# Fused attention and sparse FFN layer: another order of the first pair's row maxima, and feature products on another engine

## The chip, the cores and the metric

The kernel runs on one core of one Trainium2 chip. The metric is the device time of one execution, in microseconds; the median of three runs of the kernel before is 409.96 us (409.67 to 410.95). The engines of a core run their own instruction streams and meet at semaphores: TensorE (PE), VectorE (DVE), ScalarE (ACT), GpSimd (POOL) and SyncE (SP, here only DMA issue).

## The reference

The layer has 1024 tokens of width 256, 16 heads of 16 dimensions, and 8 "splats" per head. Attention is computed twice, with plain scores and with guided scores (plain plus a term from splat features), and the two outputs are blended. A feed-forward layer with 2:4 sparsity follows.

```python
q, k, v = heads(x @ Wq.T), heads(x @ Wk.T), heads(x @ Wv.T)
scores = einsum('bhid,bhjd->bhij', q, k) / sqrt(hd)
std_out = out_proj(softmax(where(mask, scores, neg)))
diff  = x[:, :, :, None, :] - splat_positions                # of q and of k
gauss = exp(-0.5 * sum(diff * diff, -1) / scales ** 2)
dirp  = tanh(einsum('bhsnd,hnd->bhsn', diff, dirn))
splat_attn = einsum('bhin,bhjn->bhij', amp * qg, kg) + strength * einsum(..., amp * qg * qd, kg * kd)
gsa_out = out_proj(softmax(where(mask, scores + sensitivity * splat_attn, neg)))
x = layernorm(x + (1 - blend) * std_out + blend * gsa_out)
h = silu(x @ w_gate) * (x @ w_up);  x = layernorm(x + keep_2_of_4(h) @ w_down)
```

## The kernel before

Matrix products use float32r parts: a value is split into a high part and a low part, and three products (lines 743 to 745) make one. The 16 heads are worked on in 8 pairs. A matrix of 128 rows holds 8 heads, so the first four pairs come from "chunk" 0 and the last four from chunk 1. For each chunk c, for q and k (w = 0, 1) and for both halves of the tokens (hf = 0, 1) there are a projection ("proj"), a Gaussian part ("gauss") and a directional part ("dirp"). A feature is made in five steps. PE makes gauss and dirp, ACT takes exp and tanh of them (L654, L662), DVE multiplies them (L1088 for q, with a factor, and L1091 for k), ACT rounds the product to its high part (L618) and DVE subtracts that to have the low part (L1099). Features 0 to 3 are those of chunk 0, and 4 to 7 those of chunk 1. DMAs (`stack`, L378) then put base parts and features of one head into rows of `q_st` and `k_st`: rows 0 to 64 serve the plain scores, all 115 the guided ones.

Softmax needs row maxima before the main loop may start on a pair. PE computes score blocks (L877), DVE reduces them (L1230 a full block, L1237 the block on the diagonal, with the causal mask added), for eight tiles of 128 rows, two heads and the plain (v = 0) and guided (v = 1) scores. An item ("max", pair, head, tile, piece, v, nv) is one such block, and a small one holds plain and guided together (nv = 2). The blocks go through a ring of 4 PSUM banks: PE may write a bank when DVE has read it. When all maxima of a pair are there, DVE combines them ("rows", L1215 to L1223), PE turns them ("turn_max", L883), DVE copies them (L1246), and POOL issues the DMA that puts them into `q_st` (L546, `maxima`). Then the main loop may work on the pair. It has 12 steps a pair: scores (L938), exp on ACT (L691), the causal select on POOL in steps with a diagonal (L539, `mask`), and the product with V (L912), two steps later. Maxima of the next pair are spread between its steps.

The order of the opening is written out by hand in the list `before` (lines 134 to 154). PE and DVE both walk through it: "use" entries are PE's, "read", "mul" and "lo" entries DVE's, and "max" entries both engines'. In it, the maxima of the first half (tiles 0 to 3) come after all four features of chunk 0, and PE waits for base parts and features of a head together, since both share semaphores by queue (`st_sp`, `st_pool`). The maxima of the second half (28 items) come in groups of 6, with the two matrix products of a feature of chunk 1 ahead of each group. Four products with the value weights ("v") stand between them.

In the last two pairs, POOL also splits the feed-forward weights into high and low parts (`split`, L528 and L530), 8 pieces of two instructions. They are placed in steps 4 to 7 of each of the two pairs. At step 6 POOL also does `blend_sum` (L553), for which PE's transposes of the attention output wait (L825).

## Time and profile before

| What | Value |
|---|---|
| median of three runs | 409.96 us |
| profiled execution | 409.22 us |
| its span in the trace | 407.5 us |
| PE busy | 382.9 us (94%) |
| DVE busy | 313.9 us (77%) |
| ACT busy | 230.6 us (57%) |
| POOL busy | 112.2 us (28%) |
| first scores of the main loop | 76.54 us after the span's start |

The span is what the trace covers, and the execution's own time is 1.72 us longer. Busy time of PE is modelled, since its matmuls overlap: 94% doesn't mean full speed. The page's line PEclk gives the clock that was granted to PE, in tenths of 2.4 GHz. In rows of the timeline the first number is the start, the second the duration; the part in brackets is the engine's idle time before it, with what ended it. DVE instructions overlap by some 0.08 us, so the start of the next one tells how long one holds the engine.

### The profile page before, as it was taken

Reading aid. Unit: us, or ns where it says so; the run is one execution under the profiler, and the core shown is the slowest. Engines: PE = TensorE matmul, PEld = TensorE weight load, DVE = VectorE, ACT = ScalarE, POOL = GpSimd, SP = SyncE. Lnnn points to the kernel's source line nnn. Section 1 sums busy time; section 2 is a strip of 40 time slices with the busy share of each in tenths; the row PEclk is TensorE's granted clock in tenths of the full one; section 3 lists DMA queues with packets and bytes.
Section 4 is the critical chain, followed back from the end, with each engine's and each line's share of the span. In section 5 each row is a group of like instructions: output and inputs, shape, how many; then the busy total and the mean of one; then the engine's idle time right before and its main releaser. Section 6 shows DMA issues by size and latency. Waiting matters only on the chain.

```text
span 407.5 us, 6706 instructions
## 1 busy us (share of the span) xinstructions
PE 382.9 (94%) x2234; PEld 254.4 (62%) x2234; DVE 313.9 (77%) x908; ACT 230.6 (57%) x451; POOL 112.2 (28%) x163
## 2 busy tenths in 40 slices
PE   7997886999999999999999999999879899999995
PEld 6666555765565565565565565564445388888884
DVE  2757899899889889889889889889113457999955
ACT  4964242476676676676676676676675836444100
POOL 8579200111321321321321321366475200000000
PEclk9998999799999999999999999999998999999999
DMA  6152656000360360351261257200000000000003
GB/s 206 32 101 42 102 97 98 3 2 0 55 99 10 50 98 17 48 93 20 45 98 22 44 97 237 99 2 1 5 0 2 0 2 0 0 2 0 2 0 103
DMA packets 12906, 19.69 MB, mean 48 GB/s; under 512 B 5492, under 2 KB 8564, under 8 KB 12872
## 3 DMA queue, kind: packets, MB, share of 16 engines
q1 hardware_dynamic: 10328, 18.18, 22.3%
q0 software_dynamic: 1536, 1.07, 1.6%
q8 instruction: 18, 0.29, 0.3%
q10 hardware_dynamic: 1008, 0.02, 0.1%
q14 instruction: 16, 0.13, 0.1%
HBM read 5.26 MB, written 1.05 MB: 15 GB/s over the span
## 4 chain that ended last, share of the span: by engine, by line
PE 79%; DVE 10%; ACT 6%; DMA 2%; issue 2%; SPq 1%; POOL 0%; DVEq 0%; ACTq 0%
PE ps L938 19%; PE ps L912 17%; PE ps L877 16%; PE ps L841 7%; PE ps L743 5%; PE ps L745 5%; PE ps L744 5%; DVE ps L1237 3%; PE ps L899 2%; ACT pr L691 2%; DVE mpart L1230 2%; DMA x_sb<-_attn_hidden_states_dram 2%; PE ps L825 1%; DVE gauss L1088 1%; PE ps L805 1%
## 5 line engine op out<-in xcount | busy, mean ns | idle before, releaser
L691 ACT ACTIVATE pr<-ps 128x512 f32<-128x512 f32 (+2 forms) x320 | 157.3, 561 | 81.4 <-PE ps L938 79.8
L1237 DVE CUSTOM_DVE_ANT_0 ps<-ps,causal 128x512 f32<-128x512 f32 (+3 forms) x256 | 145.7, 614 | 20.2 <-PE ps L877 18.4
L938 PE MATMUL ps<-q_st,k_st 67*128 67x512 f32 (+7 forms) x384 | 126.7, 373 | 0.4 <-DMA q_st<-m_t 0.4
L877 PE MATMUL ps<-k_st,q_st 65*128 65x512 f32 (+5 forms) x384 | 117.4, 363 | 3.6 <-DVE mpart L1237 2.1
L938 PEld LDWEIGHTS ps<-q_st,k_st 67*128 67x128 f32 (+1 forms) x384 | 68.0, 190 | 67.6 <-ACT pr L691 41.9
L912 PE MATMUL ps<-pr,vx 128*32 128x512 f32 (+3 forms) x768 | 82.5, 503 | 1.0 <-ACT o_sb L677 1.0
L877 PEld LDWEIGHTS ps<-k_st,q_st 65*128 65x128 f32 (+1 forms) x384 | 69.4, 195 | 16.1 <-DVE mpart L1237 6.1
L539 POOL TENSOR_SCALAR_AFFINE_SELECT pr<-pr 128x512 f32<-128x512 f32 x64 | 40.6, 635 | 115.8 <-ACT pr L691 115.8
L1230 DVE TENSOR_REDUCE mpart<-ps 128x2 f32<-128x256 f32 (+2 forms) x96 | 54.8, 596 | 8.3 <-PE ps L877 8.3
L1237 DVE DVE_READ_ACCUMULATOR2_ANT mpart<- 128x1 f32 x256 | 35.9, 140 | 0.0
L912 PEld LDWEIGHTS ps<-pr,vx 128*32 128x32 f32 x768 | 15.2, 108 | 23.7 <-ACT pr L691 14.8
L553 POOL TENSOR_TENSOR attn<-otmp 128x128 f32<-128x128 f32 x16 | 7.4, 462 | 62.1 <-DVE otmp L1266 62.1
L841 PE MATMUL ps<-wd,hid 128*128 128x256 f32 x96 | 21.4, 379 | 0.0
L841 PEld LDWEIGHTS ps<-wd,hid 128*128 128x128 f32 x96 | 18.2, 190 | 2.5
L728 ACT ACTIVATE sg<-ps 128x512 f32<-128x512 f32 x16 | 9.5, 597 | 14.9 <-PE ps L745 14.9
L1262 DVE RECIPROCAL rec<-ps 128x16 f32<-128x16 f32 x16 | 4.0, 253 | 18.0 <-PE ps L899 18.0
L546 POOL DMA_DIRECT2D q_st<-m_t x16 | 9.7, 608 | 27.4 <-DVE m_t L1246 27.4
L582 ACT ACTIVATE rstd<-rstd 128x4 f32<-128x4 f32 (+2 forms) x6 | 1.2, 206 | 23.6 <-DVE rstd L1185 23.5
L743 PE MATMUL ps<-yt_hi,wg_hi 128*128 128x512 f32 x32 | 12.7, 397 | 0.0
L745 PE MATMUL ps<-yt_hi,wg_lo 128*128 128x512 f32 x32 | 12.6, 394 | 0.0
L745 PE MATMUL ps<-yt_hi,wu_lo 128*128 128x512 f32 x32 | 12.6, 394 | 0.0
L744 PE MATMUL ps<-yt_lo,wu_hi 128*128 128x512 f32 x32 | 12.5, 392 | 0.0
(186 smaller groups left out, 494.2 us busy)
## 6 DMA issues: line engine op xcount, KB each, us to landing
q_st<-base_hiq SPq DMA_DIRECT2D x28, 64.0 KB
k_st<-base_hik SPq DMA_DIRECT2D x28, 64.0 KB
q_st<-feat_hiq SPq DMA_DIRECT2D x28, 64.0 KB
k_st<-feat_hik SPq DMA_DIRECT2D x28, 64.0 KB
x_sb<-_attn_hidden_states_dram SPq DMA_DIRECT2D x4, 256.0 KB, 5.3
raw<-in_L_ffn_w_gate_dram SPq DMA_DIRECT2D x1, 1024.0 KB, 4.9
raw<-in_L_ffn_w_up_dram SPq DMA_DIRECT2D x1, 1024.0 KB, 7.1
wd<-in_L_ffn_w_down_dram SPq DMA_DIRECT2D x1, 1024.0 KB, 9.1
```

Of the source, the lines that this page charges most:

```text
L539: pool.affine_select(out=pr[:, s % NP, :, d:d + P], in_=pr[:, s % NP, :, d:d + P], compare_op=ALU.is_ge, fill=0.0, base=0, pattern=[[0, 4] ...
L546: pool.dma_start(q_st[p % NB][row:row + 2, :, :].bitcast(F32), m_t[first:first + 32, p % 2, :]).then_inc(m_loaded, 16)
L691: act.activation(pr[:, s % NP, 2 * hh + vs[0]:2 * hh + vs[-1] + 1, d:BANK], src, ACT.Exp, scale=SCALE).then_inc(exp_done, 1)
L743: pe.matmul(out, lhs[0], rhs[0], start=first, stop=False, **kw)
L744: pe.matmul(out, lhs[0], rhs[1], start=False, stop=False, **kw)
L745: return pe.matmul(out, lhs[1], rhs[0], start=False, stop=last, **kw)
L841: mm = pe.matmul(ps[:, bank, 0:D], hid[u % 4][:, c, tok], wd[:, m, :], start=(m == 0), stop=(m == HC - 1))
L877: mm = pe.matmul(ps[:, slot, at:at + n], q_st[b][0:rows, hh, i * P:(i + 1) * P], k_st[b][0:rows, hh, first:first + n], start=(v == v0), st ...
L912: mm = pe.matmul(ps[32 * t:32 * t + 32, 7, off:BANK], vx[:, kt, 2 * p + t // 2, :], pr[:, s % NP, t, off:BANK], start=(kt == 0), stop=(kt ...
L938: mm = pe.matmul(ps[:, bank, j * width:(j + 1) * width], k_st[b][0:rows, hh, kt * P:(kt + 1) * P], q_st[b][0:rows, hh, q:q + width], start ...
L1230: dve.tensor_reduce(mpart[:, c, i, hh, v:v + nv], ps[:, slot, :].rearrange("p (v n) -> p v n", v=nv)[:, :, 0:n], AX, ALU.max).then_inc(rin ...
L1237: ins = dve.tensor_tensor_reduce(out=ps[:, slot, at:at + n], in0=ps[:, slot, at:at + n], in1=causal[:, BANK - n:BANK], scale=1.0, scalar=- ...
```

## The change

Four things are changed.

First, the row maxima of the first half no longer wait for all features. The plain scores of tiles 2 and 3 (4 items, `plain0`) come ahead, between the products of features 2 and 3, and the 8 items that need features (`guided0`) follow. For this, the rows of `q_st` and `k_st` have their own semaphores: `base_in` for base parts, `feat_in` for features, each by half and head. In the second half, 12 plain items come first and 16 that need features after them.

Second, POOL makes the products and low parts of features 4 to 7 (`second_feature`), after its memsets and ahead of the first DMA of maxima. The factor of q is a multiplication of its own there. DVE does features 0 to 3 only.

Third, the products with the value weights come later in PE's order, the first ahead of the last group of maxima.

Fourth, POOL's 8 splits of feed-forward weights are in steps 3 to 5 of the seventh pair and steps 3 to 7 of the eighth.

```diff
@@ -102,9 +102,9 @@
     A_FIRST = ([("xt", 0), ("xt", 1), ("wt", 0), ("wt", 1), ("xt", 2), ("xt", 3), ("proj", 0, 0, 0), ("proj", 0, 1, 0),
                 ("proj", 0, 0, 1), ("bt", 0), ("proj", 0, 1, 1)]
                + [(k, 0, w, hf) for hf in range(2) for w in range(2) for k in ("gauss", "dirp")])
-    A_LATER = ([("wt", 2), ("wt", 3)] + [("proj", 1, w, hf) for w in range(2) for hf in range(2)] + [("bt", 1), ("v", 0)]
+    A_LATER = ([("wt", 2), ("wt", 3)] + [("proj", 1, w, hf) for w in range(2) for hf in range(2)] + [("bt", 1)]
                + [(k, 1, w, hf) for w in range(2) for hf in range(2) for k in ("gauss", "dirp")]
-               + [("v", b) for b in range(1, 4)])
+               + [("v", b) for b in range(4)])
     A_USES = A_FIRST + A_LATER
     A_BANK = [n % 7 for n in range(len(A_FIRST))] + [NR + (n + 1) % NR for n in range(len(A_LATER))]
     A_READ = {"xt": "ad", "wt": "ad", "bt": "ad", "proj": "ad", "gauss": "a", "dirp": "a", "v": "a"}
...
@@ -119,27 +119,26 @@
 
         return ("d", a_index[u])
 
-    early = [it for it in row_items(0) if it[3] < TPG]
-    late = [it for it in row_items(0) if it[3] >= TPG]
-    before = ([use("wt", 2), use("wt", 3), use("proj", 1, 0, 0)] + early[:2] + [use("proj", 1, 0, 1)] + early[2:4]
-              + [read("wt", 2), read("wt", 3), read("proj", 1, 0, 0), use("proj", 1, 1, 0)] + early[4:6]
-              + [read("proj", 1, 0, 1), use("proj", 1, 1, 1)] + early[6:8]
-              + [read("proj", 1, 1, 0), use("bt", 1), use("v", 0)] + early[8:10]
-              + [read("proj", 1, 1, 1), read("bt", 1)] + early[10:])
+    def first_items(hf, needs_features):
+
+        return [it for it in row_items(0) if it[3] // TPG == hf and (it[5:] != (0, 1)) == needs_features]
+
+    plain0, guided0 = first_items(0, False), first_items(0, True)
+    late = first_items(1, False) + first_items(1, True)
+    n0 = len(guided0) // 2
+    before = ([use("wt", 2), use("wt", 3), ("mul", 2), ("lo", 2), plain0[0], ("mul", 3), plain0[1], ("lo", 3),
+               use("proj", 1, 0, 0)] + plain0[2:] + [read("wt", 2), read("wt", 3), use("proj", 1, 0, 1)] + guided0[:n0]
+              + [read("proj", 1, 0, 0), use("proj", 1, 1, 0), read("proj", 1, 0, 1)] + guided0[n0:n0 + 2]
+              + [use("proj", 1, 1, 1), use("bt", 1), read("proj", 1, 1, 0)] + guided0[n0 + 2:]
+              + [read("proj", 1, 1, 1), read("bt", 1)])
     UNIT = 6
     for n, it in enumerate(late):
         f = TPG + n // UNIT
-        if n % UNIT == 0 and f < len(features):
-            before += [use("gauss", *features[f]), use("dirp", *features[f])]
-        if n % UNIT == UNIT - 1 and f < len(features):
-            before.append(("mul", f))
-        if n % UNIT == 1 and TPG < f:
-            before.append(("lo", f - 1))
-        if n == len(late) - UNIT + 2:
-            before.append(use("v", 1))
+        if n % UNIT == 0:
+            before += [use("gauss", *features[f]), use("dirp", *features[f])] if f < len(features) else [use("v", 0)]
         before.append(it)
     nexts = stream[per_pair:per_pair + LEAD]
-    before += ([("rows", 0), use("v", 2), ("turn_max", 0)] + nexts[:LEAD // 2] + [use("v", 3)] + nexts[LEAD // 2:])
+    before += ([("rows", 0), use("v", 1), use("v", 2), ("turn_max", 0)] + nexts[:LEAD // 2] + [use("v", 3)] + nexts[LEAD // 2:])
     at_step = [[] for _ in steps]
     sent = per_pair + LEAD
     total_t, total_m = float(sum(cost_t)), float(sum(cost_m))
...
@@ -386,21 +385,21 @@
                 queue.dma_start(dst[b][row:row + HD, hh, cols].bitcast(F32),
                                 src[r:r + HD, c, cols].bitcast(F32)).then_inc(done, 16)
 
-        def first_base(queue, done, w, hf):
+        def first_base(queue, w, hf):
 
             queue.wait_ge(reused[0], 3)
             queue.wait_ge(a_act, A_ACT[a_index[("proj", 0, w, hf)] + 1])
             queue.wait_ge(a_dve, A_DVE[a_index[("proj", 0, w, hf)] + 1])
             for hh in range(2):
-                stack(queue, 0, hh, ("bq", "bk")[w], done[hf][hh], slice(hf * BANK, hf * BANK + BANK))
-
-        def first_features(queue, done, hh):
+                stack(queue, 0, hh, ("bq", "bk")[w], base_in[hf][hh], slice(hf * BANK, hf * BANK + BANK))
+
+        def first_features(queue, hh):
 
             for f in range(4):
                 _, w, hf = features[f]
                 queue.wait_ge(feat_h, f + 1)
                 queue.wait_ge(feat_l, f + 1)
-                stack(queue, 0, hh, ("fq", "fk")[w], done[hf][hh], slice(hf * BANK, hf * BANK + BANK))
+                stack(queue, 0, hh, ("fq", "fk")[w], feat_in[hf][hh], slice(hf * BANK, hf * BANK + BANK))
 
         @block.sync
         def _(sp):
...
@@ -506,13 +505,32 @@
                                pattern=[[-1, BANK]], channel_multiplier=1).then_inc(consts, 1)
             pool.memset(vx[:, :, :, HD:32], 1.0).then_inc(consts, 1)
             for w in range(2):
-                first_base(pool, st_pool, w, 1)
-            first_features(pool, st_pool, 1)
+                first_base(pool, w, 1)
+            first_features(pool, 1)
 
             pool.wait_ge(a_pe, a_index[("dirp", 0, 1, 1)] + 1)
             pool.wait_ge(feat_l, 4)
             for b in range(1, NB):
                 constant_rows(b)
+
+            def second_feature(f):
+
+                c, w, hf = features[f]
+                cols = slice(hf * BANK, hf * BANK + BANK)
+                if w == 0:
+                    pool.wait_ge(a_act, A_ACT[a_index[("gauss", c, w, hf)] + 1])
+                    pool.tensor_scalar(gaussian(c, w, cols), gaussian(c, w, cols), spk[:, c, 12:13], None,
+                                       ALU.mult).then_inc(scaled, 1)
+                    pool.wait_ge(scaled, hf + 1)
+                pool.wait_ge(a_act, A_ACT[a_index[("dirp", c, w, hf)] + 1])
+                pool.tensor_tensor(gaussian(c, w, cols), gaussian(c, w, cols), directional(c, w, cols),
+                                   ALU.mult).then_inc(feat_f, 1)
+                pool.wait_ge(feat_h, f + 1)
+                pool.tensor_tensor(feat_lo[w][:, c, cols], gaussian(c, w, cols), feat_hi[w][:, c, cols].bitcast(F32),
+                                   ALU.subtract).then_inc(feat_l, 1)
+
+            for f in range(TPG, len(features)):
+                second_feature(f)
 
 
             def slices():
...
@@ -553,6 +571,8 @@
                 pool.tensor_tensor(dst, otmp[:, :, :, 0, :], otmp[:, :, :, 1, :], ALU.add).then_inc(attn_done, 1)
 
             work = list(enumerate(slices()))
+            SPLIT_STEPS = ([(PAIRS - 2, n) for n in range(TPG - 1, 2 * TPG - 2)]
+                           + [(PAIRS - 1, n) for n in range(TPG - 1, 2 * TPG)])
             maxima(0)
             for s in range(len(steps)):
                 mask(s)
...
@@ -561,7 +581,7 @@
                         maxima(it[1])
                     elif it[0] == "turn_out":
                         blend_sum(it[1], it[2])
-                if steps[s][0] >= PAIRS - 2 and TPG <= s % SPP < 2 * TPG and work:
+                if (steps[s][0], s % SPP) in SPLIT_STEPS:
                     m, (n, src, hi, lo) = work.pop(0)
                     split(m, n, src, hi, lo)
             assert not work
...
@@ -858,15 +880,16 @@
                 if it[0] == "max":
                     _, p, hh, i, c, v0, nv = it
                     b = p % NB
-                    if p == 0 and i % TPG == 0 and c == 0 and v0 == 0:
-                        hf = i // TPG
-                        if (hf, hh) != (1, 1):
-                            pe.wait_ge(st_sp[hf][hh], 16 * (12 if hf == hh == 0 else 6))
-                        if (hf, hh) != (0, 0):
-                            pe.wait_ge(st_pool[hf][hh], 16 * (12 if hf == hh == 1 else 6))
+                    if p == 0:
+
+                        for hf in range(i // TPG + 1):
+                            for loaded in [base_in] + [feat_in] * (v0 + nv - 1):
+                                if (loaded, hf, hh) not in seen:
+                                    seen.append((loaded, hf, hh))
+                                    pe.wait_ge(loaded[hf][hh], 16 * 6)
                     elif i == 0 and v0 == 0:
                         pe.wait_ge(st_loaded[b][hh], loads(b, p // NB + 1))
-                    if i == 0 and v0 == 0:
+                    if it in (plain0[0], plain0[len(plain0) // 2]) or p > 0 and i == 0 and v0 == 0:
                         pe.wait_ge(reused[b], 3)
                     first, n, _ = row_pieces(i)[c]
                     n = max(n, HALF)
...
@@ -1151,7 +1174,7 @@
             link(dve.scalar_tensor_tensor(out=spk[:, :, 12:13], in0=spk[:, :, 3:4], scalar=sc[:, 1:2],
                                           in1=spk[:, :, 11:12], op0=ALU.mult, op1=ALU.mult))
             link(dve.tensor_scalar(spk[:, :, 12:13], spk[:, :, 12:13], 1.0 / SCALE, None, ALU.mult))
-            for f in range(4):
+            for f in range(2):
                 opening_read(a_index[("dirp", *features[f])])
                 feature_low(f)
                 if f == 0:
```

The following rows show DVE's order in the opening, from the end of the work on the first two features on. The names are those of the tiles: `gauss` the product, `feat_lo` the low part, `mpart` a row maximum, `sc` and `blend` small constants. The first column is the line, and that of the kernel after is 23 higher for the same statement. Before:

```order
L1088 SCALAR_TENSOR_TENSOR gauss<-gauss,spk,dirp 128x512
L1099 TENSOR_TENSOR feat_loq<-gauss,feat_hiq 128x512
L1091 TENSOR_TENSOR gauss<-gauss,dirp 128x512
L1099 TENSOR_TENSOR feat_lok<-gauss,feat_hik 128x512
L1159 TENSOR_SCALAR sc<-sc 128x1
L1160 RECIPROCAL sc<-sc 128x1
L1161 TENSOR_SCALAR sc<-sc 128x1
L1162 COPY blend<-sc 128x8
L1163 TENSOR_SCALAR blend<-sc 128x8
L1237 ISA ps,mpart<-ps,causal 128x128
L1237 ISA mpart 128x1
L1237 ISA ps,mpart<-ps,causal 128x128
```

And after:

```order
L1111 SCALAR_TENSOR_TENSOR gauss<-gauss,spk,dirp 128x512
L1122 TENSOR_TENSOR feat_loq<-gauss,feat_hiq 128x512
L1260 ISA ps,mpart<-ps,causal 128x384
L1260 ISA mpart 128x1
L1114 TENSOR_TENSOR gauss<-gauss,dirp 128x512
L1260 ISA ps,mpart<-ps,causal 128x512
L1260 ISA mpart 128x1
L1122 TENSOR_TENSOR feat_lok<-gauss,feat_hik 128x512
L1260 ISA ps,mpart<-ps,causal 128x384
L1260 ISA mpart 128x1
L1260 ISA ps,mpart<-ps,causal 128x512
L1260 ISA mpart 128x1
```

The constants move ahead of the third feature, and four plain maxima move between and behind the products of features 2 and 3.

The next rows are POOL's, from its memsets of `q_st` and `k_st` to the DMA of the first pair's maxima. Before:

```order
L471 MEMSET q_st 128x2048
L471 MEMSET k_st 64x2048 x2
L471 MEMSET q_st 128x2048
L471 MEMSET k_st 64x2048 x2
L546 DMA q_st<-m_t 2x16x128 x2
L539 AFFINE_SELECT pr<-pr 128x4x128 x4
```

And after:

```order
L470 MEMSET q_st 128x2048
L470 MEMSET k_st 64x2048 x2
L522 TENSOR_SCALAR gauss<-gauss,spk 128x512
L526 TENSOR_TENSOR gauss<-gauss,dirp 128x512
L529 TENSOR_TENSOR feat_loq<-gauss,feat_hiq 128x512
L522 TENSOR_SCALAR gauss<-gauss,spk 128x512
L526 TENSOR_TENSOR gauss<-gauss,dirp 128x512
L529 TENSOR_TENSOR feat_loq<-gauss,feat_hiq 128x512
L526 TENSOR_TENSOR gauss<-gauss,dirp 128x512
L529 TENSOR_TENSOR feat_lok<-gauss,feat_hik 128x512
L526 TENSOR_TENSOR gauss<-gauss,dirp 128x512
L529 TENSOR_TENSOR feat_lok<-gauss,feat_hik 128x512
```

Ten instructions, two of them with a constant factor (L522), are put between the memsets and the DMA.

The last rows are POOL's from the second `blend_sum` step of the seventh pair to that of the eighth. L553 of before is L571 of after, L528 and L530 are L546 and L548, the DMA L546 is L564, and the select L539 is L557. Before:

```order
L530 TENSOR_TENSOR wg_lo<-raw,wg_hi 128x512
L528 TENSOR_SCALAR wg_hi<-raw 128x512
L530 TENSOR_TENSOR wg_lo<-raw,wg_hi 128x512
L539 AFFINE_SELECT pr<-pr 128x4x128 x2
L546 DMA q_st<-m_t 2x16x128 x2
L539 AFFINE_SELECT pr<-pr 128x4x128 x6
L553 TENSOR_TENSOR attn<-otmp 128x4x32
L528 TENSOR_SCALAR wu_hi<-raw 128x512
L530 TENSOR_TENSOR wu_lo<-raw,wu_hi 128x512
L528 TENSOR_SCALAR wu_hi<-raw 128x512
L530 TENSOR_TENSOR wu_lo<-raw,wu_hi 128x512
L553 TENSOR_TENSOR attn<-otmp 128x4x32
```

And after:

```order
L571 TENSOR_TENSOR attn<-otmp 128x4x32
L557 AFFINE_SELECT pr<-pr 128x4x128 x2
L564 DMA q_st<-m_t 2x16x128 x2
L557 AFFINE_SELECT pr<-pr 128x4x128 x6
L571 TENSOR_TENSOR attn<-otmp 128x4x32
L546 TENSOR_SCALAR wg_hi<-raw 128x512
L548 TENSOR_TENSOR wg_lo<-raw,wg_hi 128x512
L546 TENSOR_SCALAR wu_hi<-raw 128x512
L548 TENSOR_TENSOR wu_lo<-raw,wu_hi 128x512
L546 TENSOR_SCALAR wu_hi<-raw 128x512
L548 TENSOR_TENSOR wu_lo<-raw,wu_hi 128x512
L571 TENSOR_TENSOR attn<-otmp 128x4x32
```

Ahead of the seventh pair's second group of selects (L539, L557) there were two splits, of which the rows show three instructions. There are none now, as that pair's three splits are all ahead of its `blend_sum`. In the eighth pair three splits instead of two stand between two `blend_sum`.

## Rows read from the trace of the kernel before

**Rows 1.** The page, chain that ended last, by engine.

```profile
PE 79%; DVE 10%; ACT 6%; DMA 2%; issue 2%; SPq 1%; POOL 0%; DVEq 0%; ACTq 0%
```

**Rows 2.** Busy time by stretch: stretch, length, PE PEld DVE ACT POOL, PEclk.

```profile
100.00:200.00 100.00, 100.00 (x657) 59.30 (x654) 86.83 (x285) 65.48 (x135) 24.84 (x42) 1.00 0.32 51
...
69.70:76.50 6.80, 6.77 (x27) 6.09 (x28) 4.61 (x19) 0.60 (x1) 1.24 (x2) 0.51 0.17 28
34.30:38.90 4.60, 4.56 (x13) 3.65 (x14) 3.09 (x7) 1.09 (x2) 4.43 (x4) 0.63 0.00 0
...
46.90:68.70 21.80, 17.99 (x79) 12.28 (x77) 21.33 (x53) 7.59 (x13) 0.00 (x0) 1.00 0.59 98
```

**Rows 3.** Timeline of DVE, first half: start, duration, instruction, idle before.

```profile
36.82 0.70 DVE L1237 CUSTOM_DVE_ANT_0 ps<-ps,causal 128x512 f32<-128x512 f32 x1 [1.38 <-PE ps L877]
...
39.66 0.30 DVE L1237 CUSTOM_DVE_ANT_0 ps<-ps,causal 128x128 f32<-128x128 f32 x1 [0.89 <-PE ps L877]
...
41.84 0.57 DVE L1237 CUSTOM_DVE_ANT_0 ps<-ps,causal 128x384 f32<-128x384 f32 x1 [0.27 <-PE ps L877]
...
43.77 0.28 DVE L1076 COPY bt_sq<-ps 128x128 f32<-128x128 f32 x1
...
46.98 0.42 DVE L1230 TENSOR_REDUCE mpart<-ps 128x2 f32<-128x256 f32 x1 [1.61 <-PE ps L877]
```

**Rows 4.** Timeline of DVE, second half and after it.

```profile
49.78 0.74 DVE L1088 SCALAR_TENSOR_TENSOR gauss<-gauss,spk,dirp 128x512 f32<-128x512 f32 x1
50.45 0.69 DVE L1237 CUSTOM_DVE_ANT_0 ps<-ps,causal 128x512 f32<-128x512 f32 x1
...
51.56 0.68 DVE L1099 TENSOR_TENSOR feat_loq<-gauss,feat_hiq 128x512 fp32r<-128x512 f32 x1
52.16 0.55 DVE L1230 TENSOR_REDUCE mpart<-ps 128x1 f32<-128x384 f32 x1
...
68.49 0.14 DVE L1237 DVE_READ_ACCUMULATOR2_ANT mpart<- 128x1 f32 x1
...
75.22 0.70 DVE L1237 CUSTOM_DVE_ANT_0 ps<-ps,causal 128x512 f32<-128x512 f32 x1 [1.43 <-PE ps L877]
```

**Rows 5.** Timeline of PE in the opening.

```profile
34.34 0.47 PE L743 MATMUL ps<-xt_hi,w_hi 128*128 128x512 f32 x1 [2.33 <-issue]
...
44.20 0.47 PE L743 MATMUL ps<-base_hiq,bt_hi 128*128 128x512 f32 x1 [1.75 <-DVE bt_sq L1076]
...
46.53 1.42 PE L877 MATMUL ps<-k_st,q_st 65*128 65x256 f32 x7
...
69.73 0.39 PE L883 MATMUL ps<-ident,mrow 128*64 128x128 f32 x1 [2.17 <-DVE mrow L1223]
...
76.54 0.40 PE L938 MATMUL ps<-q_st,k_st 67*128 67x512 f32 x1
```

**Rows 6.** POOL's two instructions of a split, by form.

```profile
L530 POOL TENSOR_TENSOR wu_lo<-raw,wu_hi 128x512 fp32r<-128x512 f32 x4 | 6.2, 1552 | 0.3
...
L528 POOL TENSOR_SCALAR wu_hi<-raw 128x512 fp32r<-128x512 f32 x4 | 4.5, 1127 | 0.0
```

**Rows 7.** Timeline of ACT, the high part of feature 4.

```profile
50.56 0.63 ACT L618 ACTIVATE feat_hiq<-gauss 128x512 fp32r<-128x512 f32 x1 [3.14 <-DVE gauss L1088]
```

**Rows 8.** DMA issues of maxima: count, KB each, median us to landing.

```profile
q_st<-m_t POOLq DMA_DIRECT2D x16, 16.0 KB, 2.2
```

**Rows 9.** Timeline, last maxima of the eighth pair: POOL, DVE and PE.

```profile
283.81 1.56 POOL L530 TENSOR_TENSOR wg_lo<-raw,wg_hi 128x512 fp32r<-128x512 f32 x1
283.87 1.54 DVE L1219 TENSOR_TENSOR mdiff<-mpart 128x16 f32<-128x16 f32 x1
...
286.36 0.27 PE L883 MATMUL ps<-ident,mrow 128*64 128x128 f32 x1 [1.55 <-DVE mrow L1223]
```

**Rows 10.** Timeline, eighth pair: the blend sum and who waits for it.

```profile
306.05 0.46 POOL L553 TENSOR_TENSOR attn<-otmp 128x128 f32<-128x128 f32 x1 [0.57 <-DVE otmp L1266]
...
308.51 0.60 PE L825 MATMUL ps<-ident,attn 128*128 128x128 f32 x4
```

11 lines of the change are left out of this document (6 added, 5 removed).

## Prediction

> **What bounds the kernel now.** I read the chain of waits first. PE has 79% of it [rows 1], and in the main loop it is always busy (100.00 of 100 us between 100 and 200 us, [rows 2]). So work that leaves DVE or POOL there gives nothing. What helps is an earlier start of the main loop, since nothing behind it is tied to absolute time. The loop's first scores start at 76.54 us [rows 5]. Next I read the same table for the opening. Between 46.9 and 68.7 us it is the other way round: DVE is busy for 21.33 of 21.8 us, PE for 17.99 [rows 2]. Last I read the timelines for who waits where. In the first half DVE waits 1.38, 0.89 and 0.27 us for score blocks, and 1.61 us ahead of the first block of the second half [rows 3]. PE waits 2.33, 1.75 and 2.17 us [rows 5]. After two of these waits its granted clock is low: 0.63 on average between 34.3 and 38.9 us, and 0.51 between 69.7 and 76.5 us, right ahead of the loop [rows 2]. That is mostly the lower of its two levels, 1.2 GHz. After the wait of 1.75 us it stays at 2.4 GHz.
>
> **The first half.** DVE's order changes, its work doesn't. Four plain maxima and the constants now fill waits of DVE between the products of features 2 and 3, at about 0.15 us delay to these. Behind the last low part of chunk 0, the work up to `bt_sq` is lighter by the constants (0.7 us, five small instructions) and by the two plain maxima that fit in earlier (0.52 + 0.65 us). It is heavier by the last two maxima of the second head, which stood behind `bt_sq` (1.25 us). The three waits of 2.54 us [rows 3] go, since PE gets its banks early: I laid its products and blocks out in the new order at full clock, and each block is there 0.8 us or more before DVE wants it. So `bt_sq` ends 2.54 + 0.7 + 1.17 - 1.25 - 0.15 = 3.0 us earlier, at 41.0 instead of 44.05 us [rows 3]. If PE's blocks came as late as now, 0.5 us would be left.
>
> PE, however, has nothing to do while DVE goes through its last four lower parts and maxima. It is through at about 37.0 us, and its next product needs `bt_sq`. That is an idle time of 4 us in place of 1.75 us [rows 5]. Waits of 2.33 and 2.17 us were followed by the low clock, so I expect a stretch at 1.2 GHz of about the length of the first one, 3.4 us, in the next feature products. These are 2.33 us of work (44.20 to 46.53, [rows 5]), of which some 1.3 us will come on top. The bounds are 0 (it stays at 2.4 GHz) and 2.7 us (it stays low for twice as long, as it does from 69.7 us on).
>
> **The second half.** DVE loses eight instructions. A product holds it for 0.67 us (49.78 to 50.45) or, without the factor, as long as a low part, 0.60 us (51.56 to 52.16) [rows 4]. Two by 0.67 and six by 0.60 are 4.9 us. The stretch from 46.98 to 68.63 us [rows 3, 4] is 21.65 us. Without these and some 0.4 us in which DVE isn't busy there (21.80 - 21.33 us, [rows 2]), 16.3 us of maxima are left. But the eight instructions were what DVE did while PE made the next feature products. Its ring holds four blocks, some 2.3 us of maxima, against 2.33 us of products and some 0.45 us until the first block behind them is read (46.53 to 46.98). I put 0.7 us for each of the three remaining sets, 2.1 us in all. It can't be below 0, nor above the cover that goes, 1.27 us each, so 3.8 us.
>
> So the last maximum of the first pair ends at 41.0 + 2.93 (44.05 to 46.98 as now) + 1.3 + 16.3 + 2.1 = 63.6 us instead of 68.63: 5.0 us earlier.
>
> **POOL's chain.** It starts when exp of feature 4 is there, some 43.6 us, after memsets that end there now. The nearest rows for its work are the two instructions of a weight split: 1.55 us for two inputs, 1.13 us for one [rows 6]. They read with a stride, so they should be an upper bound for contiguous tiles. Two scalings, eight operations with two inputs and four waits for ACT's high part (0.63 us, [rows 7], and signals) are 2.26 + 12.4 + 3.0 = 17.7 us, so it ends at about 61.3 us, 4 us before the DMA of the maxima must be issued. PE's value products need banks that ACT empties behind this chain, the last at about 57 us, where PE wants them after 61. It costs nothing unless it is 4 us late, a quarter longer.
>
> **From there to the loop.** Now it takes 76.54 - 68.63 = 7.9 us, with the clock at 0.51. Two of three remaining value products have moved into the wait ahead of the turned maxima, so PE has no such wait and should keep 2.4 GHz. It could then win up to 3 us, but the blocks of the next pair go through DVE, which now waits only 1.43 us for them [rows 4]. I take 1.4 us, from 0 to 2. The DMA of maxima then lands about when PE is through.
>
> **The weight splits.** At 283.81 us POOL starts the last low part of the seventh pair. DVE's subtraction of 16 columns starts at 283.87 and takes 1.54 us, to the end of POOL's instruction, and PE then waits 1.55 us for the result [rows 9]. In the new order this pair's splits are over at about 279 us, so the subtraction has no POOL instruction beside it, and I take the whole wait, 1.5 us (from 0 to 1.8). The Trainium skill, "SBUF — State Buffer", section "Who interferes with whom", says that a VectorE instruction with two SBUF inputs contends with a GpSimd instruction that reads SBUF, and one with a single SBUF input does not. The trace agrees: the subtraction has two, and took as long as POOL's. By the same rule the 28 maxima beside POOL's new chain, with one operand in PSUM, aren't slowed.
>
> In the eighth pair three splits instead of two stand ahead of `blend_sum`. From its 306.05 us [rows 10] it moves to the end of the third, 300.0 + 3 x 2.73 = 308.2 us, and ends at 308.7. PE wants it at 308.51 [rows 10]: 0.2 us lost.
>
> **Sum.** 5.0 + 1.4 + 1.5 - 0.2 = 7.7 us. The profiled execution took 409.22 us (span 407.5 plus 1.72 around it), so 401.5 us. The median is 0.74 us above it: 402.3 us.
>
> **Rivals.** (1) *The clock takes more back.* The stretch at 1.2 GHz lasts twice as long, and another falls on the start of the loop as now. For it: the second stretch of before is of that length; against it: PE's wait there goes. Then 2.7 instead of 1.3, and nothing instead of 1.4: 4.9 us gained, 405.1 us. (2) *POOL's reads still meet DVE's combining of maxima.* The chain could end 2 us late, on the combination at 63.6 us, or a split could again lie on that of the eighth pair. Each would cost what it cost at 283.87 us, about 1.5 us: 403.8 us. For it is only that POOL's times are taken from strided rows; against it the gap of 2 us and more. (3) *POOL becomes the bound, slower than before.* The DMA of maxima waits for the chain and lands 2.8 us after its start (two issues, and 2.2 us from the last, [rows 8]). With operations of d us instead of 1.55, the chain ends at 61.3 + 8 (d - 1.55) us and the loop can't start before 2.8 us later. The change would lose from 76.54 us plus the 1.3 us that the splits give back, so from a d of 3.3 us. At 3.7 us the chain ends at 78.5 us and the loop starts at 81.3: 4.8 us later, less 1.3, so 413.5 us. For it is the locking that [rows 9] show; against it that DVE has nothing with two SBUF inputs beside it. (4) *The clock is kind.* No low stretch in the second half, and the one at 304.5 to 308.5 us, which is a matter of the wait ahead of it, goes with the shift: 1.3 and 1.5 us more, 399.5 us. (5) *The change doesn't do what it says:* features of chunk 0 land late, so PE blocks in order on the guided items and DVE's waits stay. Then 2.5 us are lost: 404.8 us. Base parts are issued 3 us ahead of the features, which speaks against it.
>
> **Chances.** Forecast 0.52, (1) 0.17, (2) 0.10, (3) 0.04, (4) 0.10, (5) 0.07. The rest of each goes with its neighbours. The range from 399.3 to 406.0 us holds all but (3) and the tails. This kernel's measurement tells a change from none at about 0.3%, 1.2 us. Only (3) is on the other side of it: faster 0.94, same 0.02, slower 0.04.
>
> **What would show it.** The first scores of the loop start at about 70.2 us. `bt_sq` ends at 41 us, with PE idle for 4 us ahead of it, and PE's granted clock falls below 0.8 somewhere between 41 and 49 us. DVE waits some 0.7 us ahead of each sixth maximum. POOL's chain ends near 61 us with two-input operations of 1.1 to 1.55 us. The subtraction of 16 columns takes 0.18 us in all eight pairs, and PE's wait of 1.55 us is gone. Wrong it would be if PE waited for DMAs between 27 and 37 us, if the granted clock stayed low up to the loop, or if ACT's first exp waited for POOL.

## The result, and the profile after

The changed kernel takes 403.71 us (median of four runs, 402.72 to 404.75) against 409.9 us for the kernel before (median of four runs, 409.67 to 410.95): a ratio of 0.9837, 95% interval 0.9813 to 0.9862. Forecast were 402.3 us and a range of 399.3 to 406.0 us. The profiled execution took 403.28 us (span 401.5 us), 5.9 us less than that of before. From the page (busy time, granted clock, chain by engine):

```profile
PE 382.3 (95%) x2234; PEld 253.3 (63%) x2234; DVE 307.2 (77%) x900; ACT 231.2 (58%) x451; POOL 125.9 (31%) x173
...
PEclk9999699999999999999999999999998999999999
...
PE 84%; DVE 6%; ACT 4%; POOL 3%; DMA 2%; issue 1%; SPq 1%; DVEq 0%; ACTq 0%
```

PE now has 84% of the chain in place of 79% [rows 1]. The 6 in the clock's row, 40 to 50 us, wasn't there before. The stretches that answer to [rows 2]:

```profile
core 0: us, PE busy (x) PEld busy (x) DVE busy (x) ACT busy (x) POOL busy (x), PEclk, DMA share, GB/s
34.30:38.90 4.60, 2.64 (x13) 1.82 (x13) 4.60 (x18) 2.23 (x5) 4.43 (x4) 1.00 0.01 2
39.80:46.40 6.60, 5.68 (x12) 3.85 (x12) 1.38 (x4) 1.38 (x2) 5.23 (x4) 0.50 0.66 103
46.90:64.95 18.05, 17.07 (x81) 12.49 (x81) 15.58 (x42) 7.55 (x12) 11.62 (x9) 1.00 0.60 99
64.95:70.98 6.03, 5.76 (x38) 4.51 (x36) 5.39 (x25) 1.50 (x3) 1.31 (x2) 1.00 0.67 98
...
302.30:305.60 3.30, 3.30 (x15) 1.31 (x13) 0.16 (x1) 2.43 (x5) 3.13 (x4) 0.52 0.00 0
```

The low clock has left the stretch ahead of the loop (1.00 where 0.51 was) and the one at 34 to 39 us, and lies on the feature products, from 39.6 to 46.4 us at 1.2 GHz. DVE in the opening (start, duration, instruction, idle time before it and what ended it; compare [rows 3, 4]):

```profile
40.29 0.28 DVE L1099 COPY bt_sq<-ps 128x128 f32<-128x128 f32 x1
45.79 0.70 DVE L1260 CUSTOM_DVE_ANT_0 ps<-ps,causal 128x512 f32<-128x512 f32 x1 [5.22 <-PE ps L900]
...
50.30 0.70 DVE L1260 CUSTOM_DVE_ANT_0 ps<-ps,causal 128x512 f32<-128x512 f32 x1 [0.82 <-PE ps L900]
...
54.80 0.42 DVE L1253 TENSOR_REDUCE mpart<-ps 128x2 f32<-128x256 f32 x1 [0.80 <-PE ps L900]
...
58.96 0.69 DVE L1253 TENSOR_REDUCE mpart<-ps 128x1 f32<-128x512 f32 x1 [0.79 <-PE ps L900]
...
64.81 0.14 DVE L1260 DVE_READ_ACCUMULATOR2_ANT mpart<- 128x1 f32 x1
```

`bt_sq` ends at 40.57 us (44.05 before), the last maximum at 64.95 us (68.63 before). PE's side of it, with the start of the loop (76.54 us in [rows 5]):

```profile
40.72 0.77 PE L763 MATMUL ps<-base_hiq,bt_hi 128*128 128x512 f32 x1 [3.79 <-DVE bt_sq L1099]
...
66.06 0.27 PE L906 MATMUL ps<-ident,mrow 128*64 128x128 f32 x1
...
70.98 0.50 PE L961 MATMUL ps<-q_st,k_st 67*128 67x512 f32 x1
```

POOL's new chain, first and last feature, and the DMA behind it (L522 scales, L526 multiplies, L529 subtracts):

```profile
44.96 1.57 POOL L522 TENSOR_SCALAR gauss<-gauss,spk 128x512 f32<-128x512 f32 x1 [1.25 <-ACT gauss L674]
46.62 1.28 POOL L526 TENSOR_TENSOR gauss<-gauss,dirp 128x512 f32<-128x512 f32 x1
48.63 1.29 POOL L529 TENSOR_TENSOR feat_loq<-gauss,feat_hiq 128x512 fp32r<-128x512 f32 x1 [0.74 <-ACT feat_hiq L638]
...
61.51 1.31 POOL L529 TENSOR_TENSOR feat_lok<-gauss,feat_hik 128x512 fp32r<-128x512 f32 x1 [0.74 <-ACT feat_hik L638]
66.95 1.31 POOL L564 DMA_DIRECT2D q_st<-m_t  x2 [4.14 <-DVE m_t L1269]
```

The eighth pair, DVE's subtraction of 16 columns, and further on the blend sum and PE's wait for it (compare [rows 9, 10]):

```profile
278.10 0.18 DVE L1242 TENSOR_TENSOR mdiff<-mpart 128x16 f32<-128x16 f32 x1
```

```profile
301.02 0.46 POOL L571 TENSOR_TENSOR attn<-otmp 128x128 f32<-128x128 f32 x1
```

```profile
301.62 0.63 PE L845 MATMUL ps<-ident,attn 128*128 128x128 f32 x4 [1.63 <-POOL attn L571]
```

So the loop starts 5.56 us earlier. The subtraction takes 0.18 in place of 1.54 us, and the lead over the kernel before grows to 7.15 us (PE's first products behind its wait for `o_sb` start at 289.26 instead of 296.41 us). Then PE waits 1.63 us for the blend sum, runs at 1.2 GHz for 3.4 us, and 6.0 us of lead are left at the end.

### The profile page after: what moved, and what is told of

Read it like the earlier page. It is cut to its first block, busy times and chain, and to the rows that moved or that the text cites. A ratio compares the mean times of both kernels' runs of the same rounds, so it can differ in the third digit from the quotient of the medians.

```text
span 401.5 us, 6713 instructions
## 1 busy us (share of the span) xinstructions
PE 382.3 (95%) x2234; PEld 253.3 (63%) x2234; DVE 307.2 (77%) x900; ACT 231.2 (58%) x451; POOL 125.9 (31%) x173
## 4 chain that ended last, share of the span: by engine, by line
PE 84%; DVE 6%; ACT 4%; POOL 3%; DMA 2%; issue 1%; SPq 1%; DVEq 0%; ACTq 0%
PE ps L961 19%; PE ps L935 17%; PE ps L900 17%; PE ps L861 7%; PE ps L763 6%; PE ps L765 6%; PE ps L764 6%; DVE ps L1260 3%; PE ps L922 2%; PE ps L825 2%; ACT pr L711 2%; DMA x_sb<-_attn_hidden_states_dram 1%; PE ps L845 1%; POOL wu_lo L548 1%; DVE mpart L1253 1%
## 5 line engine op out<-in xcount | busy, mean ns | idle before, releaser
L557 POOL TENSOR_SCALAR_AFFINE_SELECT pr<-pr 128x512 f32<-128x512 f32 x64 | 40.7, 637 | 116.5 <-ACT pr L711 116.5
L900 PEld LDWEIGHTS ps<-k_st,q_st 115*128 115x128 f32 (+1 forms) x384 | 68.3, 191 | 13.9 <-DVE mpart L1260 5.5
L1253 DVE TENSOR_REDUCE mpart<-ps 128x1 f32<-128x384 f32 (+2 forms) x96 | 55.0, 597 | 8.4 <-PE ps L900 8.3
L571 POOL TENSOR_TENSOR attn<-otmp 128x128 f32<-128x128 f32 x16 | 7.4, 461 | 59.2 <-DVE otmp L1289 59.2
L763 PE MATMUL ps<-yt_hi,wu_hi 128*128 128x512 f32 x32 | 12.6, 394 | 0.0
L764 PE MATMUL ps<-yt_lo,wg_hi 128*128 128x512 f32 x32 | 12.4, 389 | 0.0
```

What stands on the lines that cost most here:

```text
L557: pool.affine_select(out=pr[:, s % NP, :, d:d + P], in_=pr[:, s % NP, :, d:d + P], compare_op=ALU.is_ge, fill=0.0, base=0, pattern=[[0, 4] ...
L763: pe.matmul(out, lhs[0], rhs[0], start=first, stop=False, **kw)
L764: pe.matmul(out, lhs[0], rhs[1], start=False, stop=False, **kw)
L900: mm = pe.matmul(ps[:, slot, at:at + n], q_st[b][0:rows, hh, i * P:(i + 1) * P], k_st[b][0:rows, hh, first:first + n], start=(v == v0), st ...
L1253: dve.tensor_reduce(mpart[:, c, i, hh, v:v + nv], ps[:, slot, :].rearrange("p (v n) -> p v n", v=nv)[:, :, 0:n], AX, ALU.max).then_inc(rin ...
```

## The experiments

The kernel before was run beside each group: median 409.29 us of 19 runs (406.85 to 411.55) beside the first four, 408.39 of 9 (406.66 to 411.29) beside the next four, 407.63 of 9 (406.54 to 411.45) beside the last four. Ratios are to these. The last eight kernels ran on one chip, and the changed kernel, run there once more (`after_again`, below), took 403.02 us.

**The split places alone.** The kernel before, with the condition that chooses the steps replaced:

```
-                if steps[s][0] >= PAIRS - 2 and TPG <= s % SPP < 2 * TPG and work:
+                if (steps[s][0], s % SPP) in SPLIT_STEPS:
```

> The kernel before, with nothing but the new places of the eight weight splits (three in the seventh pair, five in the eighth). Theory: VectorE's subtraction of 16 columns no longer meets a split, PE's wait of 1.55 us ahead of the turned maxima of the eighth pair goes, and part of it is given back at PE's transposes of the attention output, which wait for a blend sum that now stands behind three splits: 408.5 to 409.5 us, some 0.8 us below the kernel before. Rival (the splits pay nothing, all is given back): 409.9 us. Rival (the forecast's sizes, 1.5 less 0.2): 408.6 us.

407.21 us (404.1 to 408.96, 11 runs), ratio 0.9945 (0.9915 to 0.9974). Faster, by 2.1 us where the theory said 0.8; its interval holds 1.1 to 3.5 us. At equal mean clock (last section) 0.8 to 1.1 us are left, which is the theory's size. In its trace the subtraction takes 0.18 us and PE's wait at 286 us is gone. The trace shows one thing more: PE's wait of 1.75 us for `bt_sq`, after which the clock stayed at 2.4 GHz in the profile of before [rows 5], is followed by 1.2 GHz here.

```profile
43.87 0.47 PE L745 MATMUL ps<-base_hiq,bt_hi 128*128 128x512 f32 x1 [1.75 <-DVE bt_sq L1078]
```

```profile
44.40:47.70 3.30, 3.30 (x7) 1.94 (x6) 0.64 (x2) 0.69 (x1) 0.00 (x0) 0.50 0.64 104
```

**The split places undone** in the changed kernel, the same lines the other way round.

> The kernel after, with the splits where they were before. Theory: the wait of 1.63 us for the blend sum goes, the stall of the 16-column subtraction and its 1.55 us come back: between 403.5 and 404.7 us, that is 0 to 1 us above the kernel after (403.7 us). If the new places bring what I forecast (1.3 us), 405.0 us.

403.57 us (402.31 to 404.8, 5 runs), ratio 0.9855 (0.9817 to 0.9894): as fast as the changed kernel. The stall is back in its full size, and even the cast behind it is held (0.55 in place of 0.18 us):

```profile
278.21 1.53 DVE L1240 TENSOR_TENSOR mdiff<-mpart 128x16 f32<-128x16 f32 x1
279.77 0.55 DVE L1243 CAST mrow<-mdiff 128x32 fp32r<-128x32 f32 x1
```

```profile
280.69 0.27 PE L904 MATMUL ps<-ident,mrow 128*64 128x128 f32 x1 [1.54 <-DVE mrow L1244]
```

But its blend sum starts at 300.34 us and PE's transposes at 301.26 us without a wait. Within the changed kernel, the new places trade a wait of 1.54 us for one of 1.63 us. At equal mean clock they are still worth some 0.7 us (403.8 us here, 403.2 us for the changed kernel, four runs each at 0.987). The Trainium skill, "SBUF — State Buffer", section "Who interferes with whom", says that a VectorE instruction with two SBUF inputs contends with a GpSimd instruction that reads SBUF. The pair of 0.18 and 1.53 us agrees. For an instruction with one SBUF input the section makes an exception, which the prediction left out: in a 2-port mode it contends too. The cast has one such input and was held; which mode it ran in, no trace shows.

**The products back on DVE.** The changed kernel, with features 4 to 7 multiplied and split by DVE between its maxima as before:

```
+        if n % UNIT == UNIT - 1 and f < len(features):
+            before.append(("mul", f))
+        if n % UNIT == 1 and TPG < f:
+            before.append(("lo", f - 1))
...
-            for f in range(TPG, len(features)):
-                second_feature(f)
```

> The kernel after, with the products and low parts of features 4 to 7 on VectorE again, where they stood between the maxima before. Theory: VectorE gets back 4.9 us of work in the second half, of which some 2.4 us lie in its waits for PE (0.82, 0.80 and 0.79 us measured): the last maximum ends 2.5 to 3 us later, 406.4 us. Rival (VectorE's load was not what bound the second half, only the new order of the maxima helped): 403.7 us. Rival (nothing lies in the waits): 408.6 us.

405.81 us (403.98 to 407.66, 9 runs), ratio 0.9918 (0.9888 to 0.9948). In its trace the first late maximum is at 45.70 us, as after the change (45.79), so what differs comes behind it. The turned maxima stand at 70.36 instead of 66.06 us and the loop starts 4.1 us later; but this profile also has 1.2 GHz from 53.1 to 56.5 us, which the one of the changed kernel hasn't. In the median 2.1 us are lost, at equal mean clock (last section) 2.0 to 2.8 us, of some 5 us that the whole change is worth there. The splits give 0.7 to 1.1 us of these 5. So POOL's work is the largest part, and some 1.6 to 2 us are left for the new orders of maxima and value products. That is a subtraction: no run has the new orders alone.

**The clock held up.** The changed kernel, with 40 transposes of the identity in PE's wait for `bt_sq`, into a bank that the next product overwrites:

```
+                    if use == ("gauss", 1, 0, 0):
+                        for _ in range(40):
+                            pe.transpose(ps[:, bank, 0:P], ident[:], ident[:])
```

> The kernel after, with 40 transposes of the identity (whose result is overwritten) in PE's wait for bt_sq, so that PE is busy through its 3.79 us of idle time. Theory: the granted clock stays at 2.4 GHz, the first maximum of the second half starts at 43.5 instead of 45.79 us, and 2.3 us are gained: 401.4 us. Rival (the low clock doesn't come from this idle time): the clock falls all the same, 403.7 us.

401.53 us (401.48 to 402.77, 5 runs), ratio 0.9807 (0.9767 to 0.9847), as expected. The granted clock is 1.00 there:

```profile
36.00:40.00 4.00, 4.00 (x32) 3.57 (x31) 4.00 (x16) 1.41 (x4) 3.88 (x3) 1.00 0.01 2
40.00:47.00 7.00, 6.64 (x38) 4.99 (x36) 3.74 (x11) 1.38 (x2) 6.69 (x5) 1.00 0.66 103
```

The first late maximum starts at 44.72 instead of 45.79 us, and not at 43.5. Most of that miss isn't the edit's: everything is some 0.9 us late in this profile from its start on (the first copy of `bt_sq`, ahead of the edit, is at 17.72 instead of 16.83 us, and the second ends at 41.46 instead of 40.57 us). The transposes run 0.5 us past that end. From the end of `bt_sq` to the first late maximum it is 3.26 us, against 5.22 us in the changed kernel. The loop starts at 69.79 us, 1.2 us earlier. `bt_sq` is no earlier here and the clock doesn't fall: so the idle PE, and not DVE's lateness, made the stretch at 1.2 GHz.

**Real work in the gap.** Two of the value products moved there instead:

```
-              + [read("proj", 1, 1, 1), read("bt", 1)])
+              + [read("proj", 1, 1, 1), read("bt", 1), use("v", 0), use("v", 1)])
...
-    before += ([("rows", 0), use("v", 1), use("v", 2), ("turn_max", 0)] + nexts[:LEAD // 2] + [use("v", 3)] + nexts[LEAD // 2:])
+    before += ([("rows", 0), use("v", 3), ("turn_max", 0)] + nexts)
```

> The changed kernel, with two of its four value products put into PE's wait for bt_sq in the opening (real work in place of the idle 3.8 us) and taken out of the stretch behind the last maximum. Theory (PE's idle time, not DVE's lateness, made the stretch at the lower clock, and the lower clock cost 2.3 us of feature products): the granted clock stays at 1.00 between 40 and 47 us, the first late maximum starts some 2.2 us earlier, at about 43.6 to 44.8 us, and the time falls by about 2.3 us, to 401.4 us. Rival (the products in the gap make bt_sq's product or ACT's exp later by as much, and the later stretch lacks PE work, so that the clock falls there): no gain, 403.7 us. The kernel that filled the gap with needless transposes took 401.5 us; that this one takes less would show that moved work is worth more than padding.

403.6 us (403.38 to 412.15, 5 runs), ratio 0.9878 (0.9824 to 0.9931): no gain. Two of the five runs took 410.5 and 412.2 us, and the profiled one is among them: its clock is low from 66.9 to 90.8 us. Whether that comes with the edit, nothing here shows, so only its first 66 us are read. The first half of the theory holds: clock 1.00 between 40 and 47 us, the first late maximum at 43.55 us, 2.2 us earlier. Further on PE lacks work ahead of the turned maxima, and waits where it didn't, as the rival had it:

```profile
63.80 0.27 PE L906 MATMUL ps<-ident,mrow 128*64 128x128 f32 x1 [1.44 <-DVE mrow L1246]
```

The three other runs have a mean clock of 0.983, near the low end of the changed kernel's nine (0.981 to 0.991). So they seem to lose to the clock what the gap gained, but no trace of one of them shows where.

**`bt_sq` two maxima earlier.** In the first half's order:

```
-              + [use("proj", 1, 1, 1), use("bt", 1), read("proj", 1, 1, 0)] + guided0[n0 + 2:]
-              + [read("proj", 1, 1, 1), read("bt", 1)])
+              + [use("proj", 1, 1, 1), use("bt", 1), read("proj", 1, 1, 0)]
+              + [read("proj", 1, 1, 1), read("bt", 1)] + guided0[n0 + 2:])
```

> The changed kernel, with DVE reading the last direction block and bt_sq ahead of the last two maxima of the first half that need features. Theory (PE's idle time before the next feature product is DVE's queue ahead of bt_sq): bt_sq ends about 1.2 us earlier, at 39.4 us, PE waits 2.6 us in place of 3.8, and the time falls by 1.2 us less what the low clock keeps: 402.5 to 403.2 us. Rival (the length of the stretch at the lower clock doesn't depend on the idle time, and the two maxima are only moved behind it): no change, 403.7 us.

401.36 us (399.32 to 401.86, 5 runs), ratio 0.9816 (0.9766 to 0.9865). `bt_sq` ends at 39.33 us and PE waits 2.66 us. The expected 402.5 us were passed. The clock still falls, for 3.4 us (39.3 to 42.7). The first late maximum starts at 43.78 us, 2.0 us earlier than after the change. That is more than the 1.2 us that `bt_sq` came earlier, since the low stretch was half as long; whether the edit made it so stays open (next section).

**The blend sum first.** The eighth pair's splits at other steps:

```
-                           + [(PAIRS - 1, n) for n in range(TPG - 1, 2 * TPG)])
+                           + [(PAIRS - 1, n) for n in (3, 4, 6, 7, 7)])
```

> The changed kernel, with the eighth pair's five weight splits at its steps 3, 4, 6 and 7 (two at 7) in place of one at each of 3 to 7, so that two and not three of them stand ahead of the blend sum on POOL. Theory (PE's wait of 1.63 us for the blend sum is POOL's third split): the sum starts 2.7 us earlier, PE doesn't wait, and the time falls by up to 1.6 us, to about 402.2 us. Rival (another wait ends there, the turned weights or DVE's output, or the clock falls later by as much): no change, 403.7 us.

401.53 us (400.03 to 402.08, 5 runs), ratio 0.9822 (0.978 to 0.9864). POOL adds the blend 2.2 us earlier, and PE has no wait for it. The stretch at 1.2 GHz behind it, which the changed kernel had, isn't there either (clock 1.00 from 290 to 315 us). That needn't be the edit's: `combined`, with the splits at the same places, has 1.2 GHz from 295.2 to 298.6 us.

```profile
298.86 0.46 POOL L571 TENSOR_TENSOR attn<-otmp 128x128 f32<-128x128 f32 x1 [0.62 <-DVE otmp L1289]
```

```profile
299.78 0.60 PE L845 MATMUL ps<-ident,attn 128*128 128x128 f32 x4
```

**All together.** The edits of `bt_early` and `blend_first`, and of the value products one in the gap, one at the 24th maximum and one ahead of the turned maxima.

> The changed kernel with three edits at once: DVE reads bt_sq ahead of the last two maxima of the first half, one value product stands in PE's wait for bt_sq, and the eighth pair's splits are at steps 3, 4, 6, 7 and 7. Theory (the three losses are independent, 1.2 to 1.6 us each): 399.5 to 400.5 us. Rival (they share one bound, DVE's maxima of the second half or the clock): not under 401.4 us.

398.93 us (397.3 to 401.47, 5 runs), ratio 0.9773 (0.9719 to 0.9827). That is 4.1 us less than the changed kernel on the same chip, where the two edits alone gave 1.7 and 1.5 us. So they don't share one bound, as the rival had it. How independent they are the medians don't tell, since part of each is the clock (at a mean clock of 0.987 it is 401.3 against 403.2 us). The loop starts at 67.25 us.

**The same, with the product at the 24th maximum moved ahead of the turned maxima.**

```
-            before += [use("gauss", *features[f]), use("dirp", *features[f])] if f < len(features) else [use("v", 1)]
+            before += [use("gauss", *features[f]), use("dirp", *features[f])] if f < len(features) else []
...
-    before += ([("rows", 0), use("v", 2), ("turn_max", 0)] + nexts[:LEAD // 2] + [use("v", 3)] + nexts[LEAD // 2:])
+    before += ([("rows", 0), use("v", 1), use("v", 2), ("turn_max", 0)] + nexts[:LEAD // 2] + [use("v", 3)] + nexts[LEAD // 2:])
```

> The kernel with three edits at once (bt_sq ahead of the last two maxima, one value product in PE's wait for it, the eighth pair's splits at steps 3, 4, 6, 7 and 7), except that the second and third value products both stand ahead of the turned maxima and none behind the 24th maximum. Theory (the 1.44 us that PE waited there for the last maxima's combination is a wait that one more product fills, and two of five runs lost 3 to 4 us to a stretch at the lower clock behind it): no wait of PE at the turned maxima, fewer runs with a low clock, 397.3 to 399 us. Rival (the low stretches come from elsewhere, or the product that moves makes the loop later by its own 1.4 us): 399 us or more, with the same two kinds of runs.

399.03 us (397.3 to 400.52, 5 runs), ratio 0.9785 (0.9739 to 0.983). PE's wait of 1.44 us is gone, but the medians of the two don't differ, as the rival said. Its best run, the profiled one, keeps 2.4 GHz up to its last microsecond.

**More work on POOL, one scaling and three for each feature,** between the product and the low part:

```
+                for n in range(1):
+                    pool.tensor_scalar(feat_lo[w][:, c, cols], gaussian(c, w, cols), 1.0, None, ALU.mult).then_inc(padded, 1)
+                    pool.wait_ge(padded, 1 * (f - TPG) + n + 1)
```

> The changed kernel, with one more scaling of 128x512 on POOL for each of the four features of the second half (written to the low part's tile, which the subtraction then overwrites), between the product and the low part. A scaling in this chain took 1.1 to 1.6 us, 0.74 us of it lies in the wait for ACT's high part, so the chain ends some 1.6 to 3.4 us later, at 64.4 to 66.2 us, ahead of the turned maxima at 66.6 us. Theory (POOL's chain has 4.1 us to spare): nothing else moves, 403.7 us as before the edit. Rival (POOL's instructions slow VectorE or ACT down in the first pair, through the memory that they share): the maxima between 45 and 65 us take longer, and the time grows by 1 us or more.

> The changed kernel, with three more scalings of 128x512 on POOL for each of the four features of the second half. The chain grows by 12 x 1.13 to 12 x 1.57 us less 4 x 0.74 us, thus by 10.6 to 15.9 us, and has 4.1 us to spare. Theory (rival 3 of the prediction, the POOL chain as the bound, in its sum): the DMA of the maxima starts 6.5 to 11.8 us later and the loop's first scores that much later than 71 us, so 410 to 415 us, and this kernel is no faster than before the change. Rival (PE fills the wait with scores of the next pair, and the loop needs the maxima later than the prediction held): less than half of that, under 408 us.

> The changed kernel itself, for comparison on the same chip as the two with more work on POOL. Both theories: 402.3 to 404.8 us, the chain of POOL over at about 62.8 us.

With one: 403.51 us (401.98 to 404.73, 5 runs), with none, on the same chip: 403.02 us (401.89 to 403.77, 5 runs). The chain ends 2.1 us later, and the time is the same within the noise. The full blocks of maxima beside it still take 0.69 to 0.73 us. But the chain's last subtraction (63.48 to 64.79 us) now meets DVE's first combining of the maxima, which takes 0.46 instead of 0.18 us, and PE waits 0.29 us for the turned maxima, where it waited for nothing:

```profile
64.36 0.46 DVE L1243 TENSOR_TENSOR mpart<-mpart 128x16 f32<-128x16 f32 x1
```

That is the meeting of rival (2) of the prediction, at a fifth of the price that it gave. With three: 418.42 us (415.24 to 423.19, 5 runs; 417.7 us without the longest), ratio 1.0277 (1.0209 to 1.0345), above the expected 410 to 415 us. Here the chain is the bound (last subtraction, DMA of the maxima, first scores of the loop, and the clock around them):

```profile
76.41 1.26 POOL L534 TENSOR_TENSOR feat_lok<-gauss,feat_hik 128x512 fp32r<-128x512 f32 x1
77.61 1.31 POOL L569 DMA_DIRECT2D q_st<-m_t  x2
```

```profile
80.57 0.79 PE L966 MATMUL ps<-q_st,k_st 67*128 67x512 f32 x1 [8.73 <-DMA q_st<-m_t]
```

```profile
66.00:80.00 14.00, 5.59 (x38) 4.59 (x36) 6.12 (x24) 2.61 (x6) 12.42 (x10) 0.86 0.26 43
80.00:88.00 8.00, 7.43 (x20) 6.37 (x21) 5.37 (x12) 4.70 (x9) 0.92 (x2) 0.50 0.00 0
```

The loop starts 2.9 us after the chain's end, for which the prediction's rival took 2.8 us. It starts 9.6 us later than with the unchanged chain (70.98 us), and the time is 15 us longer. Part of the rest is the loop's first 9 us at 1.2 GHz (up to 89.7 us).

## Why the prediction was right, and where it was off

- **What bounds the kernel**: right. The earlier start of the loop (5.56 us) is what moved the end (6.0 us).
- **The first half**: right in size, 3.5 us for 3.0. The waits of DVE went. PE's wait of 4 us came as 3.79 us, and `keep_clock` shows that it costs something.
- **The clock behind that wait**: the stretch was foreseen, its price was not. It was sized by the 3.4 us from before and came out at 6.8 us, so it cost 2.3 us (5.22 us of idle DVE less 2.93) instead of 1.3. That much of rival (1) came true, its second half didn't: the start of the loop kept 2.4 GHz. The sizing was off by itself too: a stretch of 3.4 us at half the clock holds up 1.7 us of work, not 1.3, and one of 6.8 us can't cost 2.7 us where only 2.33 us of products stand. The seven profiles with the same wait (3.78 to 3.80 us) show both. Four have 1.2 GHz for 6.8 us, and the first late maximum starts 5.2 us after the end of `bt_sq`. Three (`splits_undone` and the two with more work on POOL) have it for 3.4 us and the maximum 4.5 us after: 1.6 us more than the 2.93. So the length isn't the edit's: the changed kernel and `pool_one_more` differ in nothing that PE does there, and have 6.8 and 3.4 us. The long ones begin 0.9 to 1.2 us before PE's first product behind the wait, the short ones 0.1 to 0.7 us after its start.
- **The second half**: waits of 0.82, 0.80 and 0.79 us, 2.4 us for the 2.1 forecast. From the first late maximum to the last, without these waits, 16.75 us instead of 16.3. The single maxima didn't become longer (the 16 of 128x512 took 0.70 us on average in before, after and `dve_products`), so POOL's reads are not the cause. The stretch did: the closing read of a maximum (0.14 us) runs beside DVE's next instruction where one follows at once, and counts in full ahead of a wait. There are more such waits now, which makes up most of the difference. Together with the clock this makes 3.7 us instead of 5.0 ahead at the last maximum, the prediction's largest miss.
- **POOL's chain**: forecast to end at 61.3, ended at 62.82 us with 4.14 us to spare. It started 1.4 us late (44.96 us for 43.6), behind feature products at the lower clock, and took 17.9 us for the 17.7 forecast. In that sum two terms were off against each other. A scaling by a column of factors took 1.57 us where 1.13 was taken from one by a constant, and two inputs took 1.28 to 1.31 where 1.55 was an upper bound. The slack was tested from both sides: 2.1 us more cost nothing, 15 us more made this the bound, as rival (3) said.
- **Turn to loop**: 1.9 us for 1.4, at a clock of 1.00, as forecast.
- **The splits**: the wait of 1.55 us went, 1.6 us. The blend sum was forecast to cost 0.2 us, and at PE's transposes that is what it cost: they start at 301.62 instead of 308.51 us, 6.89 us of the lead of 7.15. But that is luck. The forecast took the time at which PE wants the sum from before (308.51 us, [rows 10]), and there PE had just run for 3.4 us at 1.2 GHz:

```profile
305.00:308.51 3.51, 3.51 (x13) 0.98 (x12) 0.86 (x3) 1.57 (x3) 2.85 (x4) 0.51 0.00 0
```

  In the changed kernel PE came there at full clock, some 1.4 us sooner, and waited 1.63 us. The low stretch then fell behind the sum, on busy work, and there the term failed: the next products start at 306.28 instead of 312.57 us (6.29 us of lead, although before they waited 0.90 us), and 6.0 us are left at the end. So the step cost 1.1 us and not 0.2. `blend_first` shows that the wait was real and could be had back; at equal mean clock that is worth some 0.4 us.
- **The sum**: 3.7 + 1.9 + 1.6 − 1.1 = 6.1 us, against 6.0 measured in the spans and 7.7 forecast. Off were the second half with the clock ahead of it (1.3 us) and the blend sum (0.9 us), and the turn to the loop gave back 0.5. The median was 1.4 us above the forecast, inside the range.

What remains open: why the same wait is followed once by a short and once by a long low stretch, where `values_in_gap` loses what it gained, and what the new orders are worth alone.

## What to carry to other kernels

Take the time at which a consumer wants something from a stretch whose clock will be the same after the change: a wait can hide behind a slow stretch and come out when that goes. When a reordering empties an engine's queue ahead of a dependency, move real work into the gap, and count what the place that it left then lacks. An off-path engine can take on work up to the slack that the trace shows in front of its next duty, here 4.1 us (2.1 us more cost nothing measurable, 15 us more moved the end). And compare kernels at equal mean clock before a microsecond is put down to an edit.
